# The reciprocal of the softmax sums: from VectorE to GpSimd, in a vision transformer layer

## What is computed

```python
h = tok(x, W_proj, b_proj)
h = concat([cls_tok, h], axis=1)
h = h + attn(layernorm(h), wq, wk, wv, wo, w_gate, w_up)
h = h + ffn(layernorm(h), gate_w, gate_b, gate_center, w1, b1, w2, b2)

# in attn, for each expert e, causal, i - j < 64
attn = softmax(q @ k.T * 16 ** -0.5)
o = attn @ v
out_e = o @ wo[e].T
# silu(concat(out_e) @ w_gate.T) * (concat(out_e) @ w_up.T)
```

## Time and profile before

| what | value |
|---|---|
| runs | 4497.68, 4499.01, 4499.13 us, median 4499.01 |
| the profiled execution's own time | 4497.74 us |
| its span, first to last instruction | 4495.9 us |
| mean granted TensorE clock | 0.952 of full speed |
| the 32 turns | about 74 to 4050 us of the span |
| the feed-forward part | the rest, to the end |

### The profile page before, as it was taken

One profiled execution on the slowest core, in us unless ns is written; L12 is line 12 of the kernel. 1 busy time (PEld: TensorE's weight loads), 2 busy tenths in 40 slices (PEclk: granted clock), 3 DMA queues, 4 the chain that ended last, 5 costly groups with the idle time before them and its releaser, 6 DMA issues. The chain is left out here.

```text
span 4495.9 us, 119008 instructions
## 1 busy us (share of the span) xinstructions
PE 3880.3 (86%) x41326; PEld 2852.4 (63%) x41326; DVE 3491.9 (78%) x9633; ACT 3028.6 (67%) x9620; POOL 1091.6 (24%) x1496
## 2 busy tenths in 40 slices
PE   3888888888888898888888888888888888886998
PEld 2666666666666666666666666666666666664776
DVE  4888877787888888777778888887777788885665
ACT  2777766676777777676667777776667677772333
POOL 0222222222222222222222222222222222221222
PEclk7999999999999999999999999999999999997999
DMA  5122221111111222211111112222111111125664
GB/s 180 42 49 51 50 50 48 46 46 44 46 29 47 50 51 50 50 48 45 45 46 46 29 46 50 51 50 50 47 45 46 46 44 30 46 50 178 204 214 155
DMA packets 254292, 285.69 MB, mean 64 GB/s; under 512 B 69289, under 2 KB 236755, under 8 KB 244098
## 3 DMA queue, kind: packets, MB, share of 16 engines
q1 hardware_dynamic: 230242, 210.41, 18.4%
q10 hardware_dynamic: 4608, 38.73, 2.8%
q0 software_dynamic: 18912, 29.35, 1.9%
HBM read 123.49 MB, written 39.28 MB: 36 GB/s over the span
## 5 line engine op out<-in xcount | busy, mean ns | idle before, releaser
L864 ACT ACTIVATE p_s<-bank,smin 128x128 f32<-128x128 f32 (+1 forms) x6144 | 1821.6, 375 | 183.2 <-DVE smin L945 163.5
L945 DVE TENSOR_REDUCE smin<-bank 128x3 f32<-128x384 f32 (+1 forms) x2048 | 1135.5, 554 | 218.2 <-PE bank L721 189.7
L741 PE MATMUL bank<-ident_s,p_s 128*128 128x128 f32 (+1 forms) x6144 | 884.1, 253 | 28.2 <-DVE pt_f L950 7.9
L716 PE MATMUL bank<-masks_s,mask_id_s 128*128 128x384 f16 (+1 forms) x2048 | 675.3, 330 | 30.7 <-DVE qt_f L916 16.4
L741 PEld LDWEIGHTS bank<-ident_s,p_s 128*128 128x128 f32 (+1 forms) x6144 | 601.6, 142 | 138.9 <-issue 103.5
L721 PE MATMUL bank<-stacks_f 128*128 128x256 f16 (+3 forms) x4096 | 679.9, 247 | 0.0
L891 POOL TENSOR_TENSOR w_s<-o_raw 128x192 f32<-128x192 f32 (+1 forms) x512 | 306.9, 599 | 1180.1 <-DVE o_raw L938 1180.1
L249 PE MATMUL bank<-zt,wqkv_s 128*128 128x394 f16 x1920 | 411.0, 378 | 170.8 <-PEq L1008 161.5
L950 DVE TENSOR_TENSOR pt_f<-bank,pt_f 128x384 f16<-128x384 f32 x1024 | 552.7, 540 | 0.0
L855 ACT CAST pt_f<-bank 128x384 f16<-128x384 f32 x1024 | 510.8, 499 | 0.0
L721 PEld LDWEIGHTS bank<-stacks_f 128*128 128x128 f16 (+1 forms) x4096 | 431.1, 105 | 123.1
(11 more groups left out here) (130 smaller groups left out, 6283.5 us busy)
## 6 DMA issues: line engine op xcount, KB each, us to landing
stacks_f<-qt_f SPq DMA_DIRECT2D x768, 73.9 KB, 2.1
stacks_f<-kt_f SPq DMA_DIRECT2D x1536, 36.9 KB, 2.1
wx_t<-wx_d SPq DMA_DIRECT2D x36, 1344.0 KB
x_raw<-x_t_dram ACTq DMA_DIRECT2D x32, 1182.0 KB
rec_t<-rec_d SPq DMA_DIRECT2D x36, 582.0 KB, 3.9
stacks_f<-w_dram SPq DMA_DIRECT2D x2, 1536.0 KB
wx_d<-w_s SPq DMA_DIRECT2D x8, 384.0 KB
v_f<-v_f SPq DMA_DIRECT2D x192, 4.1 KB
```

Source lines behind the costliest of these rows:

```text
L716: nc.tensor.matmul(ps, mask_id_s[:, 0:rows], masks_s[:, m0:m0 + HU * kn], start=True, stop=False)
L741: mm = nc.tensor.transpose(turned[:, j * rows:j * rows + rows], p_slot(u)[:, k0:k0 + 128], ident_s[0:rows, 0:rows])
L864: ins = nc.scalar.activation(p_slot(s)[:, j * kn:j * kn + kn], bank[s % SR][0:rows, j * kn:j * kn + kn], ACT.Exp, scale=-1.0, bias=smin[0: ...
L945: nc.vector.tensor_reduce(least, ps, AX_X, ALU.min).then_inc(S["min_ready"], 1)
```

## The change

A tile of the sums' shape is filled with -1 once, ahead of the turns. In `divide`, GpSimd takes the sums to the power of -1 as soon as the copy of the window is there, ahead of its sum and its product; VectorE's reciprocal, its waits and its lag go. The waits of `divide` stay, that for `o_rcp_ready` included, which GpSimd's own power now sets.

```diff
+        minus_one = sb1("minus_one", [128, PAIR, HG, 1])
...
                 nc.vector.memset(power[:], -0.5)
+                nc.vector.memset(minus_one[:], -1.0)
...
-        LAG_OC, LAG_OR = 6, 7
+        LAG_OC = 6
...
                         pool.wait_ge(S["o_copied"], w + 1)
+                        nc.gpsimd.tensor_tensor(o_rcp[0:rows, w % 2], o_raw[0:rows, w % 2, :, :, 2 * HD:VW],
+                                                minus_one[0:rows], ALU.pow).then_inc(S["o_rcp_ready"], 1)
                         nc.gpsimd.tensor_tensor(mine, o_raw[0:rows, w % 2, :, :, 0:HD],
...
-                        w = window_at(s, LAG_OR)
-                        if w is not None:
-                            rows = ROWS[w % 2]
-                            dve.wait_ge(S["o_copied"], w + 1)
-                            if w >= 2:
-                                dve.wait_ge(S["o_ready"], w - 1)
-                            nc.vector.reciprocal(o_rcp[0:rows, w % 2], o_raw[0:rows, w % 2, :, :, 2 * HD:VW]
-                                                 ).then_inc(S["o_rcp_ready"], 1)
```

## The result

The changed kernel takes 4579.48 us (median of four runs, 4575.09 to 4579.88), the kernel before 4498.77: a ratio of 1.0178, 95% interval 1.016 to 1.0195. The profiled execution took 4575.09 us. The forecast was 4599, slower.

What follows compares the result with a forecast made beforehand. The prediction saw TensorE, VectorE and ScalarE in a ring, with scores rather than reciprocals deciding steady windows. Turn ends 78 plus queueing 23 minus 0 gain made 101 us on 4497.7: 4599 us, range 4480 to 4690.

Steps and rivals of the forecast that it cites:

- VectorE's reciprocals are off the path: Attention windows: the minimum follows the scores' end, so removing 512 reciprocals gains 0, at most 46 us.
- The steady windows hide the power up to X = 3.4: Windows come every 4.55 and 4.66 us; GpSimd's idle time covers the added power, so the steady part costs nothing.
- X: Time of one 12-element power on GpSimd, which delays each window's sum; taken as 3.3 us, bounds 0.71 to 4.14.
- The price of the power goes with the elements, with a fixed part; X = 3.3: GpSimd's power: fixed part 0.24 or 0.10 us, the rest by the element, giving 2.94 or 3.64; chance 0.45.
- The argument against a cost paid once per instruction: Powers at a turn's end: the second takes 0.75 us after the first's 0.72, so elements were taken to carry the price.
- in between: Rival: the power takes 1 to 2.5 us, its elements overlapping; 4 to 52 us lost, 4502 to 4550; chance 0.12.
- The end of a turn comes X - 0.87 late: After a turn's last window, output turning and the norm's z wait for GpSimd: 2.43 us, 32 times, 78 us.
- In 16 turns the last window queues, 23 us: Last copy comes 3.05 us after the one before, so the last power waits 1.46 us for its predecessor in 16 turns.
- the clock, which the prediction named as a possible error: TensorE's granted clock at a turn's end: longer idle may move slow stretches, by about 1.5 us; not in the total.
- The cheap power: Rival: the power takes near 0.71 us, so the time stays at 4494 to 4500 us, no change; chance 0.20.
- the bound VectorE: Rival: power cheap and VectorE the bound, so odd windows' 0.18 us come off, 46 us, 4452; chance 0.10.
- The rival of the locked-out edge copies: VectorE's edge copies in odd windows are held until GpSimd's power ends: 564 us lost, 5060; chance 0.06.

Runs made afterwards that it cites:

- e3_no_rcp: Kernel before the change with no reciprocal on any engine, the product taking the constant tile instead: 4493.46 us, ratio 0.9987.

## Why the prediction was right, and where it was not

- *VectorE's reciprocals are off the path.* Right: leaving out all of them gains 5 us, 10 by the stretches alone, and moving them gives 2 us back in the steady windows.
- *The steady windows hide the power up to X = 3.4.* Right: 67.16 us against 67.23, and fourteen powers alone cost nothing.
- *The price of the power goes with the elements, with a fixed part; X = 3.3.* The mechanism was right and the size off: 2.28 us. The failed step is the fixed part, taken as 0.10 to 0.24 us from other instructions of GpSimd; a power's own is 0.37, and each element 0.16 instead of 0.23 to 0.30. The argument against a cost paid once per instruction was too strong: more than half of the 0.69 is just that, and the "in between" rival, given 0.12, had the right X.
- *The end of a turn comes X - 0.87 late.* Right: with 2.28 it gives 1.41 us; measured 1.42 for the turning (4.14 against 2.72 after the copy) and 1.30 for the low halves. TensorE's wait and the releaser are those named.
- *In 16 turns the last window queues, 23 us.* With the measured X it would be 2.28 + 1.18 + 0.03 - 3.05 = 0.44 us each, 7 us. It happened in one turn, in which the last copy starts at 319.44, 3.05 after the one before: the power follows only behind the product of the window before, as these rows show, and the low halves start 6.45 us after the copy instead of 6.10. In the other 31 the copies are no longer 3.05 us apart, since after the change the slow stretch ahead of the last copy comes in nearly every turn.

```profile
319.96 0.51 POOL L901 TENSOR_TENSOR w_s<-w_s,o_rcp 128x192 f32<-128x192 f32 x1
320.43 2.27 POOL L893 TENSOR_TENSOR o_rcp<-o_raw,minus_one 69x12 f32<-69x12 f32 x1
```

- *The sum.* With the measured X its own terms give 1.41 x 32 = 45 us and 7 for the queue, 4550; without the queue, which came once, 4543. The 32 us more of the profiled execution come from the clock, which the prediction named as a possible error and left out of the sum. The forecast came within 20 us because the end's term and the queue's, 78 and 23 us, were too large and the clock's was missing: the sign and the place were earned, the closeness was luck.
- *The rivals.* The cheap power falls with 2.28 us, the bound VectorE with e3_no_rcp, and "in between" had the right X but, without the clock, a time of 4543. The rival of the locked-out edge copies falls by the changed kernel's own trace: one at 2167.63 lies within the power from 2166.84 to 2169.12, and the line of all 1024 keeps its duration, 0.14 us; here are the timeline and that line's row (duration in ns, least, median, most).

```profile
2166.84 2.28 POOL L893 TENSOR_TENSOR o_rcp<-o_raw,minus_one 69x12 f32<-69x12 f32 x1 [1.22 <-DVE o_raw L942]
...
2167.63 0.14 DVE L962 COPY w_s<-p_s 4x12 f32<-4x12 f32 x1
```

```profile
L962 DVE COPY w_s<-p_s x1024: 142/143/155, 120.8 to 4102.7; 4x12 f32<-4x12 f32 x171
```

## What to carry to other kernels

Look for what ends the wait behind an instruction before moving it to an idler engine: 110 us of a busy engine were worth 5, and the idle engine's 2.28 us were free in fourteen windows and made the turn 1.3 us later where the pipeline runs out. Take a price from two sizes of the same operation, never one size and another operation's fixed part. In a loop whose stages run at two clock levels, compare stage by stage with the granted clock beside it: of two kernels with the same delay one lost 39 us and the other 81.

## What was not expected of the hardware

A turn can fall in step with its slow stretches. Within the turns these last 3.41 or 6.83 us in the clock's records; the changed kernel's turn of 126.29 us is 37 times the shorter, and 29 turns running have the same three, at 66.8, 90.7 and 104.4 us behind the first copy. The faster form with fourteen powers and idle matmuls has 30 turns of 122.9 us, 36 times that length. That something holds the turn's length shows with two memsets: its end is 0.05 us later, and the turn stays at 126.30. What holds it is not shown.

And a GpSimd instruction can hold up a VectorE one that has a single input. At the end of a turn (timeline of the changed kernel, GpSimd's sum above from 2216.23 to 2216.82):

```profile
2215.03 0.17 DVE L314 TENSOR_SCALAR veps<-mv 128x2 f32<-128x2 f32 x1
...
2216.31 0.54 DVE L314 TENSOR_SCALAR veps<-mv 69x2 f32<-69x2 f32 x1
```

The first of these two lies under the power and takes its usual 0.17 us; the second falls under the sum and ends at 2216.85, 0.03 behind it. The rows of the two differ, 128 and 69, but that is not the reason: in the turn whose last power queued, the second one too lies under the power (320.43 to 322.70) and takes its usual time:

```profile
322.41 0.17 DVE L314 TENSOR_SCALAR veps<-mv 69x2 f32<-69x2 f32 x1
```

In the whole trace 31 of these instructions start under a sum, and each ends 0.02 to 0.03 us behind it; 33 lie under a power, and each takes 0.17. The Trainium skill, "SBUF — State Buffer", section "SBUF: two separate sides", has a shared port pair that one of the two engines holds for its whole instruction, against a VectorE instruction that has two inputs there or is in a two-port mode. The sum agrees with that if this instruction is in such a mode, which no run here shows; the power, which ran across the first and held nothing back, does not. Nobody waited for the 0.37 us here, since GpSimd was still at its product.
